# One-core attention and mixture-of-experts layer: the out-projection as three rounded products of split halves, and the work behind it tile by tile

## The reference, cut to what matters

```python
B, S, HID, NH, D = 2, 512, 512, 32, 16          # 1024 tokens, 32 heads of 16
h  = layernorm(x)
q, k, v = h @ w_q.T, h @ w_k.T, h @ w_v.T         # per head
attn = softmax(q @ k.T / 4) @ v
x  = x + attn @ w_o.T                             # out-projection and residual
h2 = layernorm(x)
logits = h2 @ gate_w.T                            # 8 experts
p, e = top_k(softmax(logits), 2)                  # p renormalised to 1
y  = sum over the two picks of p * (silu(h2 @ w1[e].T) * (h2 @ w3[e].T)) @ w2[e].T   # F = 800
out = x + y
```

## Time and profile before

| | us |
|---|---|
| three runs | 635.04, 628.47, 629.1 (median 629.1) |
| the profiled execution, its time | 632.78 |
| the profiled execution, its span | 631.0 |
| PE busy | 582.4 (92%) |
| DVE busy | 385.3 (61%) |
| ACT busy | 327.2 (52%) |
| POOL busy | 120.7 (19%) |

### The profile page before, as it was taken

How to read it: one execution, slowest core, us unless ns; L and a number is a source line. 1 busy time by engine, 2 the same in 40 slices (tenths; PEclk the granted TensorE clock), 3 DMA queues, 4 the chain that set the end, 5 groups by cost and what they waited for, 6 DMA issues and landing times.

```text
span 631.0 us, 10494 instructions
## 1 busy us (share of the span) xinstructions
PE 582.4 (92%) x3585; PEld 430.8 (68%) x3585; DVE 385.3 (61%) x689; ACT 327.2 (52%) x481; POOL 120.7 (19%) x137
## 2 busy tenths in 40 slices
PE   2999999999999999999936999999999999998993
PEld 2786764433333333323735999999999999998982
DVE  6714656799999999524576573818274655646140
ACT  4222125677787777862205555656474646565430
POOL 5000111000101001011003005142341507070312
PEclk9999996699999999999955999999999999999898
DMA  8180378444765720043754374656656665743203
GB/s 314 68 98 3 51 102 102 51 60 67 100 76 86 94 81 19 11 132 137 303 187 144 142 264 109 230 149 195 186 169 213 161 233 97 300 76 112 28 12 38
DMA packets 29496, 78.88 MB, mean 125 GB/s; under 512 B 8489, under 2 KB 8745, under 8 KB 24858
## 3 DMA queue, kind: packets, MB, share of 16 engines
q1 hardware_dynamic: 24474, 68.84, 41.4%
q0 software_dynamic: 4992, 9.64, 8.8%
HBM read 58.64 MB, written 9.80 MB: 108 GB/s over the span
## 4 chain that ended last, share of the span: by engine, by line
PE 47%; issue 28%; POOL 10%; DVE 8%; ACT 3%; DMA 2%; POOLq 1%; SPq 0%; ACTq 0%
PE ps_o L593 10%; PE ps L612 7%; PE ps L581 5%; DVE neg_max L1108 5%; PE ps L582 5%; PE ps L583 5%; POOL out L543 4%; PE ps_m L612 3%; PE ps L668 3%; POOL xn L525 3%; PE ps L624 2%; ACT probs_t L936 1%; POOL to_now L538 1%; DMA q_lo<-wq 1%; PE ps_m L668 1%
## 5 line engine op out<-in xcount | busy, mean ns | idle before, releaser
L936 ACT ACTIVATE probs_t<-ps 128x1024 f32<-128x1024 f32 x128 | 123.7, 1022 | 50.6 <-PE ps L624 50.6
L581 PE MATMUL ps<-xgT_hi,w_hi 128*128 128x294 f32 (+1 forms) x416 | 127.3, 306 | 5.2 <-DVE xgT_lo L1284 2.7
L583 PE MATMUL ps<-xgT_hi,w_lo 128*128 128x294 f32 (+1 forms) x416 | 126.3, 304 | 0.0
L582 PE MATMUL ps<-xgT_lo,w_hi 128*128 128x294 f32 (+1 forms) x416 | 125.6, 302 | 0.0
L1108 DVE TENSOR_REDUCE neg_max<-ps 128x1 f32<-128x512 f32 x171 | 111.5, 682 | 14.2 <-PE ps L612 11.7
L1297 DVE TENSOR_TENSOR act<-gate,ps 128x294 f32<-128x294 f32 x48 | 22.1, 461 | 105.6 <-PE ps L583 87.1
L581 PEld LDWEIGHTS ps<-xgT_hi,w_hi 128*128 128x128 f32 (+1 forms) x416 | 79.0, 190 | 5.7 <-DVE xgT_lo L1284 3.0
L582 PEld LDWEIGHTS ps<-xgT_lo,w_hi 128*128 128x128 f32 (+1 forms) x416 | 78.9, 190 | 0.0
L583 PEld LDWEIGHTS ps<-xgT_hi,w_lo 128*128 128x128 f32 (+1 forms) x416 | 78.5, 189 | 0.0
L612 PE MATMUL ps<-k_stack,q_stack 48*128 48x512 f32 x171 | 76.0, 482 | 2.5 <-issue 0.3
L593 PE MATMUL ps_o<-probs_t,v_ones 128*32 128x512 f32 x512 | 71.7, 633 | 0.3 <-ACT probs_t L936 0.3
(11 more groups left out here) (249 smaller groups left out, 951.0 us busy)
## 6 DMA issues: line engine op xcount, KB each, us to landing
w_sb<-w SPq DMA_DIRECT2D x18, 1024.0 KB
w_sb<-w SPq DMA_DIRECT2D x9, 1536.0 KB
w_sb<-w SPq DMA_DIRECT2D x9, 1152.0 KB
q_stack<-q_hi SPq DMA_DIRECT2D x32, 128.0 KB, 5.3
k_stack<-k_hi SPq DMA_DIRECT2D x32, 128.0 KB, 4.9
q_stack<-q_lo SPq DMA_DIRECT2D x16, 128.0 KB, 4.4
k_stack<-k_lo SPq DMA_DIRECT2D x16, 128.0 KB, 5.9
q_hi<-o_norm SPq DMA_DIRECT2D x16, 128.0 KB, 4.1
```

Of the source, the lines that this page charges most:

```text
L581: pe.matmul(o, x_hi, w_hi, start=start, stop=False)
L582: pe.matmul(o, x_hi, w_lo, start=False, stop=False)
L583: return pe.matmul(o, x_lo, w_hi, start=False, stop=stop)
L936: a.activation(probs_t[:, kc % 2, 2 * half:2 * half + 2, :], ps4[:, 2 * (n % 2):2 * (n % 2) + 2, :], ACT.Exp, scale=D ** -0.5).then_inc(s_ ...
```

## The change

Five things change, and only between the attention loop's last steps and the top-2.

1. The out-projection uses `three` on split halves. POOL splits the weights (four roundings and four subtractions, at group 10) and each finished chunk of `o_all` except the last (at every odd group from 1 to 13); the last chunk is rounded by ACT and subtracted by DVE. The halves lie in memory that q, k and the weights no longer need (`o_lo` over `o_all` itself).
2. The order on PE: tiles 0 and 1 go chunk by chunk between the scores of steps 14 and 15, and two chunks of tile 2 go ahead of the last quarter of `pv`. After the loop, tiles 4 and 5 wait for the last chunk, and tiles 6 and 7 come after it whole.
3. Residual, statistics, root, scaling and transposes go tile by tile (tiles 0 and 1 as a pair), tiles 0 to 2 being transposed ahead of the last chunk's landing.
4. Logits of tiles 0 to 3 and of 4 to 6: the gate's weights are padded to 32 columns and are PE's stationary operand, one chunk for each 32-column strip of the array (`chunk_logits`, the transposed tiles being the 512 moving columns, the strips placed as those of `pv`); ACT copies the four strips out, and one product per tile with a 0/1 matrix `chunk_sum` adds and turns them (`summed`). Tile 7 keeps the old form.
5. DVE takes maxima and indices of tiles 0 to 3 as soon as those are there, and of 4 to 7 after that.

The diff, cut to what the prediction speaks of:

```diff
@@ -113,13 +114,21 @@
+        tail = ExitStack()
+        o_lo = sb(tail, "o_lo", [P, NG // 2, S], f32r)
+        wo_lo = sb(tail, "wo_lo", [P, HC, HID], f32r)
+        wo_hi = sb(tail, "wo_hi", [P, HC, HID], f32r)
+        o_hi = sb(tail, "o_hi", [P, NG // 2, S], f32r)
+        xn2T = sb(tail, "xn2T", [P, NT, HC, P])
+        tail.close()
+        lg_t = q_hi[:, 0:2, :].bitcast(f32)
         xn2 = sb(ctx, "xn2", [P, NT, HID])
-        xn2T = k_lo[:, 0:4, :].bitcast(f32).rearrange("p a (c t) -> p a c t", c=HC)
         w13_sb = sb(ctx, "w13_sb", [P, W13])
...
@@ -516,6 +534,22 @@
                                    ALU.mult).then_inc(s_on, 1)
+                if g == 10:
+                    pool.wait_ge(s_wo, 16)
+                    for c in range(HC):
+                        pool.tensor_copy(wo_hi[:, c, :], wo_sb[:, c, :]).then_inc(s_woh, 1)
+                    for c in range(HC):
+                        pool.wait_ge(s_woh, c + 1)
+                        pool.tensor_tensor(wo_lo[:, c, :], wo_sb[:, c, :], wo_hi[:, c, :].bitcast(f32),
+                                           ALU.subtract).then_inc(s_wol, 1)
+                if g % 2 == 1 and g < NG - 1:
+                    c = g // 2
+                    for done in s_oc:
+                        pool.wait_ge(done, 16 * (c + 1))
+                    pool.tensor_copy(o_hi[:, c, :], o_all[:, c, :]).then_inc(s_oh, 1)
+                    pool.wait_ge(s_oh, c + 1)
+                    pool.tensor_tensor(o_lo[:, c, :], o_all[:, c, :], o_hi[:, c, :].bitcast(f32),
+                                       ALU.subtract).then_inc(s_ol, 1)
             pool.wait_ge(s_pv, TPB * NG)
...
@@ -664,22 +698,23 @@
                 b, qt = divmod(t, TPB)
+                pe.wait_ge(s_wol, HC)
+                at = slice(qt * P, (qt + 1) * P)
                 for c in range(c0, c1):
-                    last = pe.matmul(o, o_all[:, b * HC + c, qt * P:(qt + 1) * P], wo_sb[:, c, :],
-                                     start=(c == 0), stop=(c == HC - 1))
...
+                    n = b * HC + c
+                    if n < NG // 2 - 1:
+                        pe.wait_ge(s_ol, n + 1)
+                    else:
+                        pe.wait_ge(s_endl, 1)
+                    last = three(o, o_hi[:, n, at], o_lo[:, n, at], wo_hi[:, c, :], wo_lo[:, c, :], c == 0, c == HC - 1)
+                if c1 == HC:
+                    last.then_inc(s_op, 1)
+            def projection(t, c0, c1):
+                if c0 == 0:
+                    max_bank_free(pe, t, "projection")
+                project(max_bank(t, "projection"), t, c0, c1)
...
@@ -701,37 +736,70 @@
                     scores(s, 2 * p + 1)
-                    if s in (NG - 2, NG - 1) and p == 1:
-                        projection(s - (NG - 2))
-            for t in range(2, TPB):
-                projection(t)
-            packed(NG - 2)
+                    if s in (NG - 2, NG - 1):
+                        projection(s - (NG - 2), p, p + 1)
+                    elif s == NG and p == 0:
+                        projection(2, 0, HC // 2)
+            def turned(t):
+                pe.wait_ge(s_xn2, t + 1)
+                max_bank_free(pe, t, "router")
+                o = max_bank(t, "router")
+                for c in range(HC):
+                    last = pe.transpose(o[:, c * P:(c + 1) * P], xn2[:, t, c * P:(c + 1) * P], ident[:, :])
+                last.then_inc(s_t2, 1)
+            def chunk_logits(n, t0, t1):
+                pe.wait_ge(s_gw, 16)
+                pe.wait_ge(s_t2e, t1)
+                pe.wait_ge(s_res, TPB + n + 1)
+                o = ps4[:, n, 0:(t1 - t0) * P].rearrange("p (t n) -> p t n", t=t1 - t0)
+                for c in range(HC):
+                    last = pe.matmul(o[32 * c:32 * c + 32, :, :], gw_pad[:, c, :], xn2T[:, t0:t1, c, :],
+                                     start=True, stop=True, tile_position=(0, 32 * c))
+                last.then_inc(s_part, 1)
+            def summed(n, t0, t1):
+                pe.wait_ge(s_sum, 1)
+                pe.wait_ge(s_or, NG)
+                pe.wait_ge(s_partc, n + 1)
+                for t in range(t0, t1):
+                    last = pe.matmul(lg_banks[n][:, t * E:(t + 1) * E], lg_t[:, n, (t - t0) * P:(t - t0 + 1) * P],
+                                     chunk_sum[:, :], start=True, stop=True)
+                last.then_inc(s_lg, 1)
+            def logits(t):
+                pe.wait_ge(s_t2e, t + 1)
+                pe.wait_ge(s_res, TPB + 3)
+                for c in range(HC):
+                    pe.matmul(lg_banks[1][:, t * E:(t + 1) * E], xn2T[:, t, c, :], gw_pad[:, c, 0:E],
+                              start=(c == 0), stop=(c == HC - 1))
+            projection(2, HC // 2, HC)
+            projection(3, 0, HC)
             pe.wait_ge(s_ex, UNITS * NG)
-            for t in range(TPB, NT):
-                project(ps4[:, t % TPB, :], t, 0, HC - 1)
...
+            project(ps4[:, 0, :], TPB, 0, HC - 1)
+            project(ps4[:, 1, :], TPB + 1, 0, HC - 1)
+            for t in range(3):
+                turned(t)
+            project(ps4[:, 0, :], TPB, HC - 1, HC)
+            project(ps4[:, 1, :], TPB + 1, HC - 1, HC)
+            project(ps4[:, 2, :], TPB + 2, 0, HC)
+            turned(3)
+            project(ps4[:, 3, :], TPB + 3, 0, HC)
+            turned(4)
+            turned(5)
+            chunk_logits(0, 0, TPB)
+            turned(6)
+            summed(0, 0, TPB)
+            turned(7)
+            chunk_logits(1, TPB, NT - 1)
+            logits(NT - 1)
+            summed(1, TPB, NT - 1)
...
@@ -936,14 +1004,36 @@
-            for t in range(NT):
-                if t % TPB == 0:
-                    root(B + t // TPB + 1, t)
+            def turned(t):
                 a.wait_ge(s_t2, t + 1)
-                if t >= TPB:
-                    a.wait_ge(s_lg, t - TPB + 1)
-                a.activation(xn2T[:, t % TPB, :, :], max_bank(t, "router").rearrange("p (c t) -> p c t", c=HC),
+                a.activation(xn2T[:, t, :, :], max_bank(t, "router").rearrange("p (c t) -> p c t", c=HC),
                              ACT.Copy).then_inc(s_t2e, 1)
+            def parts_out(n, tiles):
+                a.wait_ge(s_part, n + 1)
+                a.activation(lg_t[:, n, 0:tiles * P], ps4[:, n, 0:tiles * P], ACT.Copy).then_inc(s_partc, 1)
+            root(B + 1, 0, 2)
+            root(B + 2, 2, 3)
+            root(B + 3, 3, 4)
+            for done in s_oc:
+                a.wait_ge(done, 16 * NG // 2)
+            a.activation(o_hi[:, NG // 2 - 1, :], o_all[:, NG // 2 - 1, :], ACT.Copy).then_inc(s_endh, 1)
+            for t in range(3):
+                turned(t)
+            root(B + 4, 4, 5)
+            root(B + 5, 5, 6)
+            turned(3)
+            root(B + 6, 6, 7)
+            turned(4)
+            turned(5)
+            parts_out(0, TPB)
+            root(B + 7, 7, 8)
+            turned(6)
+            turned(7)
+            parts_out(1, TPB - 1)
             a.wait_ge(s_lsh, 1)
...
@@ -1136,6 +1226,26 @@
+            def spread(t0, t1):
+                v.wait_ge(s_res, t1)
+                for t in range(t0, t1):
+                    ins = v.bn_stats(stats[:, t, :], x1[:, t, :])
+                link(ins)
+                for t in range(t0, t1):
+                    ins = v.bn_aggr(aggr[:, t, :], stats[:, t, :])
+                link(ins)
+                v.tensor_scalar(rstd[:, t0:t1], aggr[:, t0:t1, 1], EPS, None, ALU.add).then_inc(s_var, 1)
+                norms[0] += 1
+            def scaled(t0, t1):
+                v.wait_ge(s_std, norms[0])
+                link(v.reciprocal(rstd[:, t0:t1], rstd[:, t0:t1]))
+                for t in range(t0, t1):
+                    v.tensor_scalar(xn2[:, t, :], x1[:, t, :], aggr[:, t, 0:1], rstd[:, t:t + 1],
+                                    ALU.subtract, ALU.mult).then_inc(s_xn2, 1)
...
@@ -1147,30 +1257,47 @@
                         v.reciprocal(sum_rec[:, g % 2, :], sum_rec[:, g % 2, :]).then_inc(s_rc, 1)
-                        if s in (NG - 1, NG):
-                            residual(s - (NG - 1))
+                        if s == NG - 1:
+                            residual(0)
+                            v.tensor_reduce(chunk_sum[:, :], ident[:, :].rearrange("p (c k) -> p c k", c=HC)[:, :, 0:E]
+                                            .rearrange("p c e -> p e c"), AX.X, ALU.max).then_inc(s_sum, 1)
+                        elif s == NG:
+                            residual(1)
+                            spread(0, 2)
+                        elif s == NG + 1:
+                            scaled(0, 2)
+                            residual(2)
                     if u2 == 11 and g >= 0:
-            for b in range(B):
-                for t in range(b * TPB, (b + 1) * TPB):
-                    if t >= 2:
-                        residual(t)
-                v.wait_ge(s_res, (b + 1) * TPB)
```

(30 more changed lines are left out.)

50 lines of the change are left out of this document (15 added, 35 removed).

## The result

**The change made the kernel faster: 620.92 us, median of 6 runs (620.73 to 624.23), against 629.62 for the kernel before (6 runs, 628.47 to 635.94). The ratio is 0.986, 95% interval [0.983, 0.990].** The prediction was 620.8 us, 616.5 to 626, with 0.70 on faster. The sum was nearly right; its steps were not all, and misses offset each other in part. The profile after is of the slowest of the six runs, 624.23 us.

The account below looks back on a forecast made before the run. PE alone was taken to bound the stretch from the last `pv` to DVE's maxima. Maxima 7.4 us earlier plus 0.9 for the first half made -8.3, from 629.1 to 620.8 us, range 616.5 to 626.

Parts of the forecast that it names:

- The end of attention: Steps 14 and 15 to last `pv`: -1.8 cheaper tiles, -1.6 PE waits gone, +1.4 tile 2's products; -2.0 us.
- the array changes: PE switching between 49-row scores and 128-row products, eight times more; counted as nothing, 0.8 us if 0.1 each.
- POOL's splits: Halves made on POOL during attention: rounding 0.9 us, subtraction 1.28, hidden behind DVE's maxima if POOL keeps up.
- rival 2: POOL's rounding at 3 us each makes group 11 late; 3 to 4 us reach attention's end, 624.5; chance 0.08.
- The last group's chain: Last `o_norm` move issued 1.6 us earlier, bounded by group 14's move on SP; PE then idle 1.6 us.
- Behind the last chunk: DVE 2.6 us a tile, PE 2.7; last out-projection 303.4, last scaling 307.9; DVE sets the end by a little.
- The 3.1 us from there to the maxima: Last scaling to second half's maxima, 307.9 to 311.0: transposes 0.5, copy 0.6, logits 0.9, sums 0.7, semaphores 0.4.
- The half of maxima and indices: DVE's maxima and indices for tiles 0 to 3 done before the second half's maxima start: -0.9 us.
- Rival 1: PE's clock falls in the tail for a while: 623.5 after the idle, 622.8 behind 303, both 626; chance 0.17.
- The rule of the Trainium skill: Frequent small idles between product groups can swing PE's clock; the tail would run partly at 1.2 GHz; not in the sum.
- rival 5: Array changes and semaphores eat attention's gain, DVE tiles go at 3 us: -5, 624; chance 0.08.
- Rivals 3 and 4: 3: weights' load holds the experts' start, 625, chance 0.05. 4: clock stays down from attention's end, 634, chance 0.05.

Follow-up runs that it names:

- the second pair of traces: Kernel before and changed kernel run and profiled once more, no edit; 621.59 us changed against 629.35 before, ratio 0.988.
- early load: Loads of `x` issued in steps 12 and 13 instead of 14 and 15; changed kernel 619.74 us (0.984 of before), kernel before 630.15 (0.999).
- whole tiles: Changed kernel with out-projections of tiles 0 and 1 in one piece each and nothing of tile 2 ahead of the last `pv`; 620.99 us.
- both together: Changed kernel with `x` loaded two steps earlier and tiles 0 and 1 in one piece each; 619.66 us, 0.980 of before.
- after again: The changed kernel, no edit, run and profiled a second time; 621.59 us against 629.35 for before, ratio 0.988.
- fill: Changed kernel with tile 6's first three chunks (nine products) moved into PE's wait ahead of the last chunk; 622.51 us.
- old logits: Changed kernel without strips, every tile's logits as four products of 8 columns; 625.86 us, 0.993 of before.
- norm of four tiles: Changed kernel with sequence 1's norm made for four tiles at once, as before the change; 629.43 us against 630.02, ratio 0.997.
- the same kept busy: The fill's edit plus two unused 512-column products ahead of the transposes of each of tiles 5 to 7; 620.94 us, 0.983 of before.

## Why the prediction was right, and where it was not

**The end of attention: -2.0 predicted, -1.1 measured.** The prediction's sum was -1.8 - 1.6 + 1.4; by the second pair of traces it is -0.1 - 2.5 + 1.6. ACT's waits of 3.34 us went, as said. The piece was mis-sized: in the timeline above it takes 0.89 us (268.47 to 269.36), not 0.7. Eight pieces at 0.2 more each are 1.5 us, which ate nearly all of the 1.8. What they pay for is taken to be the array changes that the prediction named and let cost nothing, with 0.8 at most; a whole tile, which has fewer of them, took 2.97 us, four pieces 3.57. The six products of tile 2 took 1.6. Against that PE lost some 2.5 us of waits (what is left of the -1.1 once the other two are taken out), where the prediction counted 1.7 in the trace and took 1.6 of them as gone. PE's own work came out 1.9 us dearer than in the sum, the waits gave 0.9 more, and the miss of 0.9 is what the two leave.

**POOL's splits: hidden, as said.** Rounding 128x512 on POOL took 0.61 us, not 0.9; the subtraction 1.28, as said:

```profile
152.14 0.61 POOL L549 CAST o_hi<-q_hi 128x512 fp32r<-128x512 f32 x1 [7.09 <-DMA q_hi<-o_norm]
152.83 1.28 POOL L551 TENSOR_TENSOR o_lo<-q_hi,o_hi 128x512 fp32r<-128x512 f32 x1
155.10 1.28 POOL L535 TENSOR_TENSOR o_norm<-o_raw,rec_all 128x512 f32<-128x512 f32 x1 [0.99 <-DVE rec_all L1274]
```

POOL waited 7.09 us for the landing in front of it, where the prediction had 2.6 "somewhat more". The next `o_norm` then still waited 0.99 us for DVE, the least of all odd groups. At the 3 us per rounding of rival 2 it would have been late.

**The last group's chain: -1.6 predicted, +0.3 measured. This is the step that failed.** The bound was the right one: `rec_row` of group 15 goes out behind group 14's move. But the prediction took the shuffle of group 14 at its old time, and it came later: at 151.6 and 151.8, where the two profiles of before have 150.2 and 150.8. With it the move of group 14 was issued at 153.8 to 153.9, where the prediction's sum has 152.9, and the last move at 158.7 to 158.8 for 156.9. What delayed the shuffle starts at the first piece on PE, ahead of the transpose of the maxima: 0.8 us on the shuffle of group 12. The two loads of `x` hand that on, because each goes out behind a group's move and the next `rec_row` behind it: a `rec_row` issued right behind a load takes 4.7 to 5.2 us to its shuffle in group 14, one with no load ahead of it 2.2 (group 13 with the early load). What is left of the delay of group 14's shuffle, 0.2 to 0.6, lies in that spread and in the small `chunk_sum` that stands ahead of group 13's shuffle on DVE (0.13). The prediction gave none of these a cost. Moving the loads gave 1.3 us of the last move back, whole tiles 0.6, both together 1.6; then the move follows the end of `pv` at 6.8 us, where before has 6.7. Even so it comes 1.3 us earlier than in before and not 1.6, since `pv` itself ends only 1.4 earlier. PE's new wait came to 2.4 to 2.5 us, predicted 1.6.

**Behind the last chunk: mis-sized, in the other direction.** DVE was predicted at 2.6 us a tile, from durations added up. The residuals of two tiles start 2.28 apart; after again, DVE:

```profile
297.10 0.69 DVE L1226 TENSOR_TENSOR x<-ps,x 128x512 f32<-128x512 f32 x1
297.71 0.15 DVE L1244 RECIPROCAL rstd<-rstd 128x1 f32<-128x1 f32 x1
...
299.38 0.69 DVE L1226 TENSOR_TENSOR x<-ps,x 128x512 f32<-128x512 f32 x1
```

A duration of 0.69 is a distance of 0.61 to the next start; the ends overlap. So the last scaling stands 3.5 us behind the last out-projection, not 4.5. That gave back 1.0 of what the chain lost, and PE, not DVE, set the pace: DVE waited for it 0.53 us ahead of residual 4 and 0.25 ahead of residual 7. The 3.1 us from there to the maxima were 3.2. The half of maxima and indices came free, -0.9 as said.

**Rival 1, the clock.** It fell in the first profile after, for nine products, and cost 1.6 us where the prediction gave 2.7; in the second it did not, with PE's wait 0.16 us longer. So the forecast and the first rival each held in one of two profiled executions. Of the other runs of after, 620.7 to 624.2 us, no trace tells which had it. The rule of the Trainium skill that the prediction weighed ("TensorE: Matmul & The Clock Gate", section "A second HAM failure mode: psum-queue depth-cycling") is borne out in part: with short idles between PE's groups the clock fell in the fill, whose waits were 0.5 us, and held in after again, whose waits there were 0.2. The falls behind the last chunk came after one wait of 2.4 to 2.7 us, which is another case. Of rival 5 the array changes came, 1.5 us of PE and hidden for the most part by waits that went. Rivals 3 and 4 did not happen: what follows the indices is the same length in the four profiles of before and after, and no profile has the clock down from the end of attention on.

**The sum** was -8.3. The stage gave -7.3 at full clock, and the medians 8.7 and 7.8 less than before in the two comparisons. That the median was met to 0.1 us is luck: the stage missed by 1.0, and the early stretch at half clock moves single runs by several.

## What to carry to other kernels

When a change moves the start of a chain forward, look for what comes last then: a bound that was hidden takes over. Here the last group hung on the end of `pv` before and on the move of the group ahead of it after, and two loads that had cost nothing, in the same queue as the chain's moves, cost 1.2 us. Work by tile beside PE can be worth more than giving PE less: the norm by tile takes nothing off PE, and the changed kernel lost more without it than without the split. And take distances between starts from the timeline, not sums of durations, when several short instructions follow each other on one engine.

## What the runs showed of the hardware that was not expected

- PE's clock fell to half right behind a wait of 2.38 to 2.65 us in three profiles (after, old logits, norm of four tiles) and did not behind one of 2.54 (after again). Behind waits of 0.3 to 1.3 us at the same place (fill, the same kept busy, whole tiles, early load) it fell in none.
- It also fell with PE busy without a gap, in or right behind 8-column products: 6.83 us for 32 in the old logits, nearly all at half clock, and 3.52 and 3.83 for 32 in the two profiles of the kernel before, where it fell towards their end.
- The stretch at half clock in the early part of the program lasted 20.5 us in the first profile of before, 10.2 in the next, and 6.8 to 13.7 in the others. With it the first `o_norm` moved between 130.2 and 135.1 us.
- In an unbroken run, three rounded products for a chunk of 128x512 took 3 x 0.23 = 0.69 us, the float32 one 0.87 (24 of them lie between 286.88 and 307.68 in the earlier trace rows): the split saves PE a fifth.
